# The order of PE's work inside an attention block: scores, value products, then all four maxima

## The reference

```
attn = einsum('bhqd,bhkd->bhqk', q * scale, k)          # first attention: + rel_h + rel_w
attn = softmax(attn, axis=-1)
out  = einsum('bhqk,bhkd->bhqd', attn, v)
```

## Time and profile before

| | us |
|---|---|
| median of 3 runs | 3566.92 |
| the profiled execution, device time | 3567.99 |
| its span in the trace | 3566.4 |
| PE busy | 2999.4 (84%) |
| DVE busy | 2460.8 (69%) |
| ACT busy | 1857.8 (52%) |
| mean granted TensorE clock over the span | 0.877 |

### The profile page before, as it was taken

The page is one execution under the profiler, slowest core; times in us unless marked ns, Lnnn a source line. Parts: engine busy times, 40 slices in busy tenths (PEclk is TensorE's granted clock), DMA queues, the critical chain, the costliest instruction groups (busy, mean ns, idle before and its releaser), DMA issues. The chain is left out here.

```text
span 3566.4 us, 65082 instructions
## 1 busy us (share of the span) xinstructions
PE 2999.4 (84%) x17813; PEld 1218.8 (34%) x17814; DVE 2460.8 (69%) x4482; ACT 1857.8 (52%) x2383; POOL 1035.9 (29%) x1684
## 2 busy tenths in 40 slices
PE   4999299999999999987886999999999995430777
PEld 3778122222222222225661222222222221430666
DVE  3443199898899988943546999999999992430211
ACT  2333047666666666672340777777777774100332
POOL 0000223333333333313212333333333321242555
PEclk9666579999999999997895999999999998555877
DMA  4655625554544445524754222222222224703211
GB/s 92 176 169 156 135 55 105 107 103 98 100 98 100 100 99 99 105 55 112 199 139 96 66 67 66 66 66 65 66 66 66 66 55 111 112 18 61 53 49 35
DMA packets 303082, 325.71 MB, mean 91 GB/s; under 512 B 148784, under 2 KB 235645, under 8 KB 298377
## 3 DMA queue, kind: packets, MB, share of 16 engines
q0 software_dynamic: 76544, 192.13, 24.3%
q1 hardware_dynamic: 190346, 119.79, 13.2%
q10 hardware_dynamic: 36096, 12.60, 2.2%
HBM read 217.71 MB, written 109.19 MB: 92 GB/s over the span
## 5 line engine op out<-in xcount | busy, mean ns | idle before, releaser
L487 DVE TENSOR_REDUCE a_halfmax<-a_psR 128x1 f32<-128x512 f32 x3072 | 1963.6, 686 | 213.9 <-PE a_psR L342 195.7
L442 ACT ACTIVATE a_probs<-a_psS 128x1024 f32<-128x1024 f32 x1536 | 1488.3, 1021 | 814.8 <-PE a_psS L360 810.7
L360 PE MATMUL a_psS<-a_qrows,a_krows 121*128 121x512 f16 (+1 forms) x3072 | 805.4, 384 | 55.4 <-DMA a_qrows<-relh 51.2
L371 PE MATMUL a_psO<-a_probs,a_v 128*32 128x512 f32 x6144 | 829.3, 612 | 1.2 <-ACT a_probs L442 1.2
L342 PE MATMUL a_psR<-a_kmax,a_qmax 64*128 64x512 f16 x3072 | 685.7, 400 | 99.5 <-DMA a_krows<-in_onehot 62.8
L342 PEld LDWEIGHTS a_psR<-a_kmax,a_qmax 64*128 64x128 f16 x3072 | 161.2, 93 | 1092.5 <-DVE a_halfmax L487 951.6
L360 PEld LDWEIGHTS a_psS<-a_qrows,a_krows 121*128 121x128 f16 (+1 forms) x3072 | 242.6, 98 | 427.9 <-issue 158.7
L203 POOL DMA_DIRECT2D a_qmax<-qk x240 | 122.2, 509 | 700.7 <-PE a_psO L371 601.7
L187 POOL DMA_DIRECT2D a_qrows<-qk x240 | 123.6, 515 | 276.5 <-PE a_psO L371 257.2
L811 PE MATMUL p_psQ<-p_xnT,p_wqk 96*128 96x512 f32 x384 | 184.7, 645 | 14.3 <-DVE p_xnT L964 12.2
L371 PEld LDWEIGHTS a_psO<-a_probs,a_v 128*32 128x32 f32 x6144 | 121.5, 108 | 184.4 <-issue 177.0
(11 more groups left out here) (157 smaller groups left out, 2261.8 us busy)
## 6 DMA issues: line engine op xcount, KB each, us to landing
a_qrows<-qk POOLq DMA_DIRECT2D x240, 128.0 KB, 3.8
qk<-p_half SPq DMA_DIRECT2D x96, 256.0 KB, 3.3
v<-p_v SPq DMA_DIRECT2D x48, 512.0 KB, 6.2
a_qrows<-rel POOLq DMA_DIRECT2D x96, 256.0 KB, 4.5
a_v<-v POOLq DMA_DIRECT2D x96, 256.0 KB, 3.1
a_krows<-qk POOLq DMA_DIRECT2D x168, 128.0 KB, 3.7
a_qmax<-qk POOLq DMA_DIRECT2D x288, 64.0 KB, 2.3
a_kmax<-qk POOLq DMA_DIRECT2D x240, 64.0 KB, 2.3
```

Of the source, the lines that this page charges most:

```text
L360: mm = nc.tensor.matmul(psS[:, (2 * n + j) % 4, :], K[buf][:, h, keys], A[buf][kt % NA][:, h, queries], start=True, stop=True)
L371: mm = nc.tensor.matmul(psO[32 * h:32 * h + 32, :], V[buf][:, kt, h, :], PT[:, blk % 2, h, :], start=(kt == 0), stop=(kt == KT - 1))
L442: nc.scalar.activation(PT[:, blk % 2, 2 * pair:2 * pair + 2, :], psS[:, b0:b0 + 2, :], ACT.Exp, scale=scale).then_inc(exped, 1)
L487: nc.vector.tensor_reduce(mx[:, unit, half:half + 1], psR[:, slot, :], AX.X, ALU.max)\
```

## The change

In each block the value products of the block before are moved ahead of the first two jobs, so that all jobs of a block stand together behind them:

```diff
@@ -397,9 +397,8 @@
 
                     scores_pair(u, kt, qh, 0, 2 * blk, 2 * blks)
                     scores_pair(u, kt, qh, 1, 2 * blk + 1, 2 * blks)
-                    some(js[:2])
                     last_pv()
-                    some(js[2:])
+                    some(js)
                 if last and u == 1:
                     pv(u, BLK - 1, blks, halves)
                     for jn, j in jobs[u][BLK]:
```

## The result

The changed kernel takes 4143.38 us in the median (4131.39 to 4159.67, 4 runs); the kernel before, timed with it, 3563.98 us. The ratio is 1.163, 95% interval 1.1586 to 1.1674. Its profiled execution has a device time of 4144.81 us and a span of 4143.2, 577 more than before.

The account below looks back on a forecast made before the run. PE was taken to set the pace of the old 2.61 us block. Onto 3567.99 us came +620 + 14 - 6 + 16 - 65 = +579, which is 4147, stated as 4145; 80% range 4095 to 4260.

Parts of the forecast that it names:

- The bound: In the old block of 2.61 us PE sets the pace; DVE's four reductions need 2.44.
- The gain of a changeover: In each block PE changes kind of matmul three times instead of four: -0.10 us.
- The chain: In each block the fourth maximum waits for the first's reduction, starting 1.17 us after it; block 3.46, 0.85 more.
- "back": Extra job in 45 blocks per attention waits for the second maximum's slot: +0.77 against +0.62 before, +7 us per attention.
- "rows": Extra job, third in its block, lies inside the fourth maximum's wait: nothing to be seen in the sum.
- DVE's share in a2: DVE's busy share in the second attention falls from 94% to about 73%.
- Waits in a1: In the first attention, waits for `relh` rows and half clock after some: 65 of 70 us gone, between 40 and 70.
- The start at half clock: Both attentions begin their steps at half clock, which may rise later: +8 us each, between 2 and 25.
- The clock in the steps: Granted clock in the second attention stays at 1.00, with no fall in the sum.
- the clock's: Rival: pauses in every block bring PE's clock down; about 4950 us if half of the time; chance 0.09.
- The rival on the other side: The fourth maximum's wait costs nothing, only the changeover counts: block 2.51 us, kernel 3495; chance 0.03.

Follow-up runs that it names:

- experiment 5: Old order with three maxima in a block instead of four, the first of each four left out: 3515.57 us, ratio 0.988 to the kernel before.
- experiment 6: New order with three maxima in a block, the first of each four left out: 3548.84 us, ratio 0.997 to the kernel before.
- experiment 1: Changed kernel with DVE reducing only 256 of the 512 columns of each maximum: 3857.12 us, ratio 1.084 to the kernel before.
- experiment 4: Changed kernel with DVE reducing the first maximum's slot twice, within the steps only: 5225.21 us, ratio 1.467.
- experiment 11: Changed kernel with the operands of a2's scores filled with zero rows from 65 to 128: 4115.43 us, ratio 1.157.
- experiment 9: Changed kernel with POOL's loads in a1 spread, rows for maxima and for scores alternating by block: 4143.87 us, ratio 1.165.
- experiment 7: New order with three maxima in a block, "back" and "rows" moved between scores and value products: 3452.77 us, ratio 0.971.
- experiment 10: Kernel of experiment 4 with the operands of a2's scores filled with zero rows from 65 to 128: 4619.36 us, ratio 1.299.
- experiment 2: Changed kernel with one maximum ahead of the value products and three behind them: 3741.56 us, ratio 1.051.

## Why the prediction was right, point by point

The forecast was 4145 us, the median is 4143.38.

- *The bound.* PE sets the pace of the old block: shown by experiment 5.
- *The gain of a changeover*, 0.10 by the sum: 0.11 in experiments 5 and 6, with nothing else in the way.
- *The chain* 0.42 + 0.69 + 0.06 until m3: 1.17 in the trace, to the hundredth; the block 3.46, as forecast. Experiments 1 and 4 shorten and lengthen one link, DVE's reduction, and the block goes along (3.19 and 4.05).
- *"back"*: the wait before it is there, 0.21, and its block takes 4.23; "rows" 4.05, +0.86 on 3.19 as on a plain block. Both as in the sum. What I wrote of "rows" was not quite right: as the third job it makes m2 the fourth, so m2 has the wait of 0.57 and m3 a second one of 0.21.
- *DVE's share in a2*: forecast about 73%, measured 70%; four reductions of 0.61 in 3.46 are 70%.
- *Waits in a1*: 65 of the 70 us gone by the sum, all 70 by the measurement: no matmul waits for `relh`, and a1 (1353) is as long as a2 is without falls of the clock (1354, experiment 11).
- *The start at half clock*: mis-sized. I took +8 for each attention. In a1 the clock rose in the second block: 3.75 and 4.80 us, 1.6 above two plain blocks, where before it was 3.1 (3.75 and 4.55). In a2 the first blocks took 3.76, 5.62, 5.62, 5.62 and 5.32, 8.6 above five plain ones, where before it was 3.9 (3.75, 4.76 and 3.24). So the change cost a1 -1.5 and a2 +4.7, not 8 each. My term priced both alike, and they aren't alike (below).
- *The clock in the steps*: I put no fall into the sum for a2. The profiled run has two, behind block 13 of two steps; a2 took 16 us more than with zero rows, 6 of them at its start, so the two falls cost about 10. So the total rests on small errors that cancel: a1 came out 16 lower than its sum (+241 against +257), a2 6 higher (+328 against +322), the rest 7 higher. The mechanism was right; that the total is within 2 us is luck.

The falls show in this timeline of PE, around block 13 of a2 in the changed kernel:

```profile
2767.27 0.39 PE L342 MATMUL a_psR<-a_kmax,a_qmax 64*128 64x512 f16 x2
2767.59 0.28 PE L346 MATMUL a_psR<-a_ident,a_rowmax 128*32 128x128 f32 x1
2768.44 0.39 PE L342 MATMUL a_psR<-a_kmax,a_qmax 64*128 64x512 f16 x1 [0.57 <-DVE a_halfmax L486]
2769.04 0.39 PE L342 MATMUL a_psR<-a_kmax,a_qmax 64*128 64x512 f16 x1 [0.21 <-DVE a_halfmax L486]
2769.36 1.04 PE L360 MATMUL a_psS<-a_qrows,a_krows 65*128 65x512 f16 x4
2770.33 1.78 PE L371 MATMUL a_psO<-a_probs,a_v 128*32 128x512 f32 x8
2772.04 1.03 PE L342 MATMUL a_psR<-a_kmax,a_qmax 64*128 64x512 f16 x3
```

Two waits in a row, 0.57 and 0.21, and the value products that begin 1.3 us later last 1.78 instead of 1.06. I had written that "rows" shows nothing in the sum; in the length of its block that is so, but it is the place where the clock goes. It happened in 2 of the 22 such blocks of a2. The profile of experiment 9, whose a2 has the same code, has two more in its 22, one of them five blocks long, and again behind block 13. a1, with its 121 rows, has none in either profile. Two waits in a row are not enough by themselves, since a block with "back" has the same 0.57 and 0.21, and none of those lost the clock; which part of block 13 does it was not tried.

Of the rivals, the clock's (0.09) was nearer than I thought: one more reduction in the chain, 0.61 us, makes it come true in a2 (experiment 4). The Trainium skill's "A second HAM failure mode: psum-queue depth-cycling", in "TensorE: Matmul & The Clock Gate", tells of a kernel whose short idle times between groups of matmuls let the clock swing between its two levels. The trace of experiment 4 agrees in a2, with 0.58 at pauses of 0.96 to 1.17 us; that of the changed kernel agrees only in those two falls. The rival on the other side was priced rightly (2.51 forecast, 2.50 measured) and its condition named rightly, one slot more than the ring has: experiments 5 to 7 meet it by taking one job away.

## What to carry to other kernels

Before jobs that share a ring are grouped, count them against its slots: up to that number a group saves a changeover (0.11 us here), and the first one beyond makes the producer wait in its own program order for the whole way of matmul, reduction and hand-over (1.17 us here), with all that is queued behind. Count every job that uses the ring, the rare ones too; they undid the gain in experiment 6. A longer block can hide a wait elsewhere, here 70 us for DMA, which is a hint that this wait can be had for itself: a first other arrangement of the loads took 1.5% off the kernel without touching PE's order, a second one, with zero rows in a2, 0.8%.

## What the runs showed of the hardware that I had not expected

In these runs TensorE's granted clock depended on how many rows of the array the scores' matmuls use, zeros included. With the same order of work and the same columns, scores of 65 rows left it at 0.58 and scores of 128 rows, 63 of them zero, at 0.97 (experiments 4 and 10); a1 with 121 rows had 0.96. At the start of a2's steps in the new order the full clock came in the fifth block in one profile with 65 rows and in the third in another (experiment 9), and in the second with 128. What was not tried is whether rows help in the maxima too, which use 64 rows at a time.

A pair of maxima in different halves of the array's rows runs as one: one alone takes 0.32 until the next kind of work, two take 0.32 as well, three 0.53 (experiment 2 and rows 3).
